# Attention and experts on one core: the first key unit of a chunk one slot ahead, and a reordered prologue

## What is computed

```python
x = x + _L0_xattn_ref(_layernorm(x), ctx, ctx, mask, Wq, bq, Wk, bk, Wv, bv, Wo, bo)
x = x + _L0_ffn_ref(_layernorm(x), Wr, W1, b1, W2, b2)

# attention
q = (q_in @ Wq + bq).reshape(bs, q_len, h, d).transpose(0, 2, 1, 3)
k = (k_in @ Wk + bk).reshape(bs, k_len, h, d).transpose(0, 2, 1, 3)
v = (v_in @ Wv + bv).reshape(bs, k_len, h, d).transpose(0, 2, 1, 3)
score = einsum('bhqd,bhkd->bhqk', q, k) / sqrt(d)
attn = softmax(where(mask, -1e+30, score))
out = einsum('bhqk,bhkd->bhqd', attn, v) @ Wo + bo

# experts
probs = softmax(einsum('bsd,ed->bse', x, Wr))
topv, topi = top_k(probs, 2)
out = sum over e of combine[e] * (gelu(x @ W1[e] + b1[e]) @ W2[e] + b2[e])
```

## Time and profile before

| | us |
|---|---|
| median of 3 runs | 906.77 |
| lowest, highest | 905.45, 907.99 |
| the profiled execution | 904.83 |
| its span | 903.0 |
| TensorE busy | 760.7 (84%) |
| VectorE busy | 670.0 (74%) |
| ScalarE busy | 621.2 (69%) |
| GpSimd busy | 477.3 (53%) |
| mean TensorE clock granted, as a share of full | 0.943 |

### The profile page before, as it was taken

The page is one execution under the profiler, slowest core; times in us unless marked ns, Lnnn a source line. Parts: engine busy times, 40 slices in busy tenths (PEclk is TensorE's granted clock), DMA queues, the critical chain, the costliest instruction groups (busy, mean ns, idle before and its releaser), DMA issues.

```text
span 903.0 us, 19629 instructions
## 1 busy us (share of the span) xinstructions
PE 760.7 (84%) x5606; PEld 546.5 (61%) x5606; DVE 670.0 (74%) x2133; ACT 621.2 (69%) x1131; POOL 477.3 (53%) x715
## 2 busy tenths in 40 slices
PE   2689899998998988889988889759999999999700
PEld 1456555655655655656665665448888888888500
DVE  3568888888888887888887887557777777777536
ACT  4667677677677676667776677458888888888500
POOL 4122665565565565454453453453777777767720
PEclk9599999999999999999999999759999999999955
DMA  5333355455445445334243233388877777877059
GB/s 157 75 83 73 98 129 150 115 135 153 115 127 154 116 130 145 102 93 100 72 100 92 70 85 80 141 281 274 253 250 236 254 240 244 243 225 246 19 205 353
DMA packets 117887, 140.33 MB, mean 155 GB/s; under 512 B 20431, under 2 KB 76134, under 8 KB 117799
## 3 DMA queue, kind: packets, MB, share of 16 engines
q1 hardware_dynamic: 105079, 115.72, 45.6%
q0 software_dynamic: 9088, 17.07, 5.4%
q10 hardware_dynamic: 3632, 6.49, 1.9%
HBM read 73.40 MB, written 36.08 MB: 121 GB/s over the span
## 4 chain that ended last, share of the span: by engine, by line
PE 52%; DMA 14%; DVE 13%; SPq 10%; ACT 4%; issue 4%; POOL 1%; POOLq 0%; DVEq 0%; ACTq 0%
DMA kb<-ks 9%; SPq L346 9%; PE bank L1247 6%; DVE mx L700 5%; PE bank L1269 4%; PE bank L1415 4%; PE bank L1412 4%; PE bank L1429 4%; PE bank L1413 4%; PE bank L1427 4%; PE bank L1428 4%; PE bank L1229 3%; DVE ks L695 3%; DMA qb<-yd 3%; PE bank L1257 2%
## 5 line engine op out<-in xcount | busy, mean ns | idle before, releaser
L630 POOL DMA_INDIRECT yd<-vs,idt x156 | 164.9, 1057 | 79.5 <-DVE vs L978 41.0
L1048 ACT ACTIVATE pt<-bank,mpair 120x512 f32<-120x512 f32 x256 | 172.2, 688 | 42.5 <-PE bank L1257 42.3
L531 POOL DMA_INDIRECT xd<-rows,posi x128 | 130.6, 1020 | 127.4 <-DVE posi L777 73.0
L700 DVE TENSOR_REDUCE mx<-bank 128x4 f32<-128x480 f32 x256 | 157.7, 648 | 38.4 <-PE bank L1247 38.2
L964 DVE TENSOR_TENSOR qb<-hid,qb 128x512 fp32r<-128x512 f32 x156 | 109.4, 702 | 68.3 <-ACT hid L1164 67.0
L1161 ACT ACTIVATE qb<-bank,btile 128x512 fp32r<-128x512 f32 x156 | 107.6, 690 | 34.0 <-PE bank L1429 25.0
L1247 PE MATMUL bank<-kb,qs 128*128 128x480 f32 x256 | 96.7, 431 | 35.9 <-DMA kb<-ks 24.9
L1269 PE MATMUL bank<-pt,vs 120*32 120x128 f32 x2048 | 111.4, 290 | 13.3 <-ACT pt L1048 10.3
L1257 PE MATMUL bank<-qb,ks 128*120 128x512 f32 x256 | 118.3, 482 | 2.6 <-DMA qb<-negm 2.6
L1164 ACT ACTIVATE hid<-bank,btile 128x512 f32<-128x512 f32 x156 | 106.3, 681 | 0.0
L1247 PEld LDWEIGHTS bank<-kb,qs 128*128 128x128 f32 x256 | 47.3, 194 | 72.0 <-DMA kb<-ks 34.5
(11 more groups left out here) (200 smaller groups left out, 1940.1 us busy)
## 6 DMA issues: line engine op xcount, KB each, us to landing
kb<-wd SPq DMA_DIRECT2D x40, 512.0 KB, 5.1
qb<-wd SPq DMA_DIRECT2D x38, 512.0 KB, 5.0
qb<-qs SPq DMA_DIRECT2D x128, 112.0 KB
kb<-ks SPq DMA_DIRECT2D x128, 105.0 KB
rows<-xd SPq DMA_DIRECT2D x39, 264.0 KB, 2.8
wd<-wsp SPq DMA_DIRECT2D x16, 512.0 KB, 3.8
qb<-yd SPq DMA_DIRECT2D x16, 512.0 KB, 6.0
xd<-zrows SPq DMA_DIRECT2D x8, 528.0 KB, 4.6
```

The costliest lines, as they stand in the source:

```text
L531: g.indirect_dma_start(xd, bass.IndirectOffsetOnAxis(ap=posi[r.phase][:, bk:bk + 1], axis=0), rows[r.phase][:, bk // 2, bk % 2, :], None, ...
L630: g.indirect_dma_start(yd, bass.IndirectOffsetOnAxis(ap=idt[k][:, j:j + 1], axis=0), yrow[p.parity][:, j, :], None, bounds_check=2 * NTOK ...
L700: v.tensor_reduce(mx[:, b, gg, :], wide[(4 + u) % 3][:, 0:J * KL].rearrange("p (j k) -> p j k", j=J), op=ALU.max, axis=AX.X).then_inc(w_fr ...
L1048: a.activation(pt[t % NP][:].rearrange("p j q -> p (j q)"), scores[t % 2][0:KL, :], ACT.Exp, bias=mpair[s.parity][:, t // G:t // G + 1], s ...
```

## The change

**Unit 0 one slot ahead.** Key unit 0 of chunk n+2 is projected at the end of slot n, behind the last `weigh` and ahead of the transpose of the maxima. ScalarE halves it at the end of slot n too, ahead of `take_heads` of sequence 1. VectorE subtracts it behind the negated maxima and ahead of the router's top 2, with a wait for the last `by_key`, since `ks` of that parity is read there. Units 1 to 3 stay. Slot -1 does this for chunk 1; chunk 0 has both key units in slot -2.

**Prologue.** TensorE projects both key units of chunk 0 ahead of the first transposes of x. ScalarE splits the key weights ahead of issuing the zero DMA of kb, then clears qb of parity 0, norms, halves unit 0, lays out the query weights, halves unit 1. The clearing of the other pair moves from the end of slot -1 to ahead of its `norm_x`. VectorE folds the biases first, subtracts unit 0, and only then prepares the masks. SyncE loads the biases ahead of the mask. GpSimd's constants (`fill`) move from the start of slot -1 to slot -2, behind the split of the context.

SyncE, prologue:

```diff
             load_x(At(0, 0))
             load_ctx(At(0, 0))
-            sp.dma_start(masku[:, :], mask).then_inc(mask_in, 16)
             for k, b in enumerate((bq, bk)):
                 sp.dma_start(bqk[:, k, :], b.rearrange("(a n) -> a n", a=1).to_broadcast([P, D])).then_inc(bias_in, 16)
+            sp.dma_start(masku[:, :], mask).then_inc(mask_in, 16)
```

GpSimd, its slot:

```diff
-                if n == -1:
-                    fill()
...
                     g.tensor_tensor(xcTl[k][:, tc], xcT[k][:, tc], xcTh[k][:, tc], ALU.subtract).then_inc(hl_done, 1)
+                    if n == -2:
+                        fill()
```

VectorE, its slot (`unsplit` now takes the chunk as an argument and stands outside `slot`):

```diff
                 if exists(n, 1):
-                    unsplit(0)
                     route(1)
-                    unsplit(1)
+                    if n != -1:
+                        unsplit(c, 1)
...
                     v.scalar_tensor_tensor(negm[k][:, 1, :], nsrc, -1.0, negm[k][:, 0, :], ALU.mult, ALU.subtract).then_inc(nm_split, 1)
+                if exists(n, 2) and n >= -1:
+                    if n >= 0:
+                        dve.wait_ge(b_full, s.count(8, 8))
+                    unsplit(c + 1, 0)
```

VectorE ahead of the slots, where the mask instructions move from ahead of the biases to behind the first new line:

```diff
+            unsplit(At(0, 0), 0)
             dve.wait_ge(mask_in, 32)
...
             v.tensor_tensor(wq3[1][:], wst[1][:], wq3[0][:], ALU.subtract).then_inc(prep, 1)
+            unsplit(At(0, 0), 1)
```

ScalarE ahead of the slots (the lines that lay out and split the query weights move to between the two new halvings):

```diff
+            act.wait_ge(wk_in, 16)
+            a.activation(wk3[0][:], wst[0], ACT.Copy).then_inc(wst_hi, 1)
             act.wait_ge(zero_src, 1)
             dst, src = clear(kb[0], "p g j n")
             act.dma_start(dst.bitcast(F32), src).then_inc(kb_zero, 16)
-            act.wait_ge(wk_in, 16)
-            a.activation(wk3[0][:], wst[0], ACT.Copy).then_inc(wst_hi, 1)
...
+            a.activation(*clear(qb[0], "p b g j q"), ACT.Copy).then_inc(blk_zero, 1)
...
             norm_x(At(-1, 1), -3)
+            halve(At(0, 0), 0, -1)
...
+            halve(At(0, 0), 1, -1)
             slots(act, slot)
```

ScalarE, its slot:

```diff
-                if exists(n, 1):
-                    halve(c, 0, n)
+                if exists(n, 1) and n != -1:
                     halve(c, 1, n)
...
+                        if n == -1:
+                            a.activation(*clear(kb[1], "p g j n"), ACT.Copy).then_inc(blk_zero, 1)
+                            a.activation(*clear(qb[1], "p b g j q"), ACT.Copy).then_inc(blk_zero, 1)
                         if exists(n, 3):
                             norm_x(s, n)
...
+                if exists(n, 2) and n >= -1:
+                    halve(c + 1, 0, n + 1)
                 if exists(n, 0):
                     take_heads(s, 1, n)
```

TensorE, its slot:

```diff
-                if exists(n, 1):
-                    project(c, 0, n)
+                if n == -2:
+                    project(s + 2, 0, -1)
+                    project(s + 2, 1, -1)
...
-                if exists(n, 1):
+                if exists(n, 1) and n != -1:
                     project(c, 1, n)
...
+                    if exists(n, 2) and n >= -1 and t == 7:
+                        project(c + 1, 0, n + 1)
                     if exists(n, 1) and t == 7:
                         pe.wait_ge(w_free, c.count(12, 12))
```

More of the change, by code:

```diff
@@ L674, in residual, with unsplit @@
                 v.tensor_tensor(xb, small[1][:, 0:D], xb, ALU.add).then_inc(x1_done, 1)
+            def unsplit(c, u):
+                k = c.parity
+                dve.wait_ge(w_part, c.count(4, u + 1))
+                gs = slice(2 * (u % 2), 2 * (u % 2) + 2)
+                if u < 2:
+                    views = ks[k][:, gs, :], *(w[:, 0:2 * KW].rearrange("p (g n) -> p g n", g=2)[:, :, 0:K2]
+                                               for w in (wide[u % 3], part[u % 2]))
+                else:
+                    views = qs[k][:, :, gs, :], *(w[:, 0:2 * N2].rearrange("p (g b q) -> p b g q", g=2, b=2)
+                                                  for w in (wide[u % 3], part[u % 2]))
+                v.tensor_tensor(*views, ALU.subtract).then_inc(w_free, 1)
             def slot(s, n):
@@ L683, in slot @@
                     dve.wait_ge(pv_done, s.count(8))
-                def unsplit(u):
-                    dve.wait_ge(w_part, c.count(4, u + 1))
-                    gs = slice(2 * (u % 2), 2 * (u % 2) + 2)
-                    if u < 2:
-                        views = ks[k][:, gs, :], *(w[:, 0:2 * KW].rearrange("p (g n) -> p g n", g=2)[:, :, 0:K2]
-                                                   for w in (wide[u % 3], part[u % 2]))
-                    else:
-                        views = qs[k][:, :, gs, :], *(w[:, 0:2 * N2].rearrange("p (g b q) -> p b g q", g=2, b=2)
-                                                      for w in (wide[u % 3], part[u % 2]))
-                    v.tensor_tensor(*views, ALU.subtract).then_inc(w_free, 1)
                 def best(u):
@@ L823, in slot @@
                 if exists(n, 1):
-                    unsplit(2)
-                    unsplit(3)
+                    unsplit(c, 2)
+                    unsplit(c, 3)
                 if exists(n, 2):
@@ L908, in _ @@
             v.tensor_tensor(wk3[1][:], wst[0][:], wk3[0][:], ALU.subtract).then_inc(prep, 1)
-            dve.wait_ge(mask_in, 32)
-            put(v.tensor_copy(maskg[:, :], masku[:, :]))
-            put(v.tensor_copy(mcol[:, :], maskuT[:, :]))
             dve.wait_ge(bias_in, 32)
@@ L1147, in _ @@
             norm_x(At(-1, 1), -3)
+            halve(At(0, 0), 0, -1)
+            act.wait_ge(wst_zero, 1)
+            act.wait_ge(z_done, 1)
+            zsrc = zq[:].rearrange("p (h d) -> p h d", h=H)
+            for c in range(3):
+                a.activation(wst[1][:].rearrange("p g j r -> p (g j) r")[:, :, 8 * c:8 * c + 8], zsrc, ACT.Copy).then_inc(wst_done, 1)
+            a.activation(wst[1][:].rearrange("p g j r -> p (g j) r")[:, :, BLO:BHI + 1],
+                         zk[:].rearrange("p (h d) -> p h d", d=1).to_broadcast([P, H, 2]), ACT.Copy).then_inc(wst_done, 1)
+            act.wait_ge(wst_done, 4)
+            a.activation(wq3[0][:], wst[1][:], ACT.Copy).then_inc(wst_hi, 1)
+            halve(At(0, 0), 1, -1)
             slots(act, slot)
```

22 lines of the change are left out of this document (6 added, 16 removed).

## The result

Beside each other on one chip, the changed kernel took 933.12 us (median of 4, 930.73 to 935.19) and the kernel before 906.11 (median of 4, 904.01 to 907.99). The ratio is 1.0287, with a 95% interval of 1.0243 to 1.0331. The profiled execution took 930.73, with a span of 928.9 (before 904.83 and 903.0). The prediction was 925 with a range of 911 to 936: the direction is right, the size is 8 us short.

What follows compares the result with a forecast made beforehand. TensorE is busy through almost all of a slot, so its waits count, the largest for the key blocks. 904.8 - 9.0 (prologue) + 27.1 (loop) = 922.9, plus 1.9 for the median, 924.8, said as 925; range 911 to 936.

Steps and rivals of the forecast that it cites:

- the chain and the step that lengthens it: Slot boundary: head transposes, key unit 1, halving, subtraction, key DMAs, max matmul; ots behind unit 0's halving delays it 0.93 us.
- The five terms: From attention matmuls' end to head transposes: unit 0, halving's start, next ScalarE instruction, ots, transposes' start; 2.43 us against 1.50.
- The plain slot: Loop slot without GpSimd's weight split; the forecast for a usual slot was 0.93 less 0.05, 0.88 us longer.
- The rival in which half is given back: Loop: the wait for key blocks shrinks and returns 0.4 to 0.6 us per boundary; 913 us, chance 0.15.
- the hold: GpSimd's weight split blocking VectorE in 16 slots: 0.4 us longer or shorter each, 6.9 in all, counted as zero.
- The prediction's sentence by that rule: In slots with a weight split, the next two-input VectorE instruction would be caught instead; sum some 7 us higher.
- the prologue: Start of the kernel through slot 0: keys projected earlier and clearing moved; 9.0 us less, bounds 7 and 11.
- Unit 0 of chunk 1: Prologue: it stands ahead of the next maxima transpose at half clock and takes back 0.4 us.
- slot 0's: Slot 0: maxima to attention matmuls 2.1 us less, from there to max matmul 0 to 2.4 less; 3.2 taken.
- the prediction's upper bound of 0.15: Loop: VectorE's subtraction of unit 0 makes the heads late; counted at nothing, at most 0.15 us per slot.
- the rival "more is lost": Loop: GpSimd's mask copy late, port lost in 16 slots, or TensorE's clock lower; 7 to 14 us more, chance 0.2.
- The prediction's rival for the intended gain: Loop: key DMAs leave earlier and the wait for key blocks goes; another 18 us less, 880, chance 0.04.

Runs made afterwards that it cites:

- Experiment 3: The kernel before, with only ots of sequence 1 copied later, behind the next slot's first halving; 1011.04 us in one run.
- Experiments 5: The changed kernel with GpSimd's weight split moved from ahead of the row copies to behind them; 956.67 us, 1.020 times the kernel before.
- experiment 9: The kernel before with the new prologue only, and GpSimd's weight split moved behind a slot's fourth scatter; 895.56 us, 0.988 times the kernel before.
- experiment 10: The new prologue with the loop of the kernel before, run a second time; 898.96 us, 0.9925 times the kernel before.
- experiment 2: The new prologue with the loop of the kernel before, first run; 943.66 us beside 948.01 for the kernel before.
- experiment 7: The changed kernel with ots copied ahead of the halving and VectorE's subtraction of unit 0 back in the next slot; 943.03 us in one run.
- experiment 1: The changed kernel with ots of sequence 1 copied ahead of the halving of unit 0; 962.03 us, 1.016 times the kernel before.

## Why the prediction came out as it did

**Right: the chain and the step that lengthens it.** The forecast named the head transposes as the point at which both paths begin, and the halving of unit 0 ahead of ots as what delays them. The five terms sum to 2.43; measured is 2.40. The wait for ots was to be some 0.9, and is 0.96. The plain slot was to be 0.88 longer, and is 17.26 less 16.38, 0.88. The terms hold one by one too: the halving starts 1.02 after unit 0 (0.98 said), ots 0.65 behind it (0.62), takes 0.59 (0.60), and the transposes follow 0.14 later (0.23). Experiment 3 shows the one-for-one rule with nothing but ots moved. The rival in which half is given back is out: the wait for the key blocks fell by 1.5 us over the whole run.

**Right by its bound, wrong in the sum: the hold.** The step read "in the sum it is zero", with 6.9 us as its bound; measured are 5.3, 0.33 in each of 16 slots. I knew from the earlier trace rows that an operation in 16 slots was held, and estimated that the split moves 0.4 later against the maxima. It moved 0.50 later (1.41 less 0.91). The step that failed is to call that a toss-up. It could have been a gain only if the end of GpSimd's subtraction did not set the slot, and the trace of before shows that it did: 13 slots at 17.11 to 17.17, wherever yy fell in the subtraction. So the 0.50 goes into the slot, less what VectorE has less to do behind the hold. Where yy is held, the extra over the 0.88 is 0.48. Where `before` is held instead, it is 0.33. Experiments 5 and 9 show that this hold is a cost of the split's place.
The Trainium skill's page "SBUF — State Buffer", section "Who interferes with whom", says that whoever comes first keeps the shared pair for its whole instruction, and that two inputs from SBUF are enough for VectorE to need it. The trace agrees in all 16 split slots of the changed kernel: each has one such operation that ends with GpSimd's subtraction. The prediction's sentence by that rule, some 7 us more, was nearer than its own zero, but not by its route: the slots in which the next operation is caught (18.33) are shorter than those in which yy is (18.48).

**Mis-sized: the prologue.** 9.0 was predicted and 6.9 measured, just under its lower bound of 7. The first max matmul is 5.6 earlier (6.2 said): the second norm starts at 16.83 and the DMA issue follows at 18.18, not 17.6. Unit 0 of chunk 1 cost 0.3 (0.4 said). The term that failed is slot 0's, 3.2 said and 1.6 measured. Its first half held (5.15 where 5.1 was said). Its second, "3.9 at full clock, as slot 1 has it", did not: the key blocks landed 6.27 after their issue, and that stretch took 5.23. That is 1.1 less than before, as much as the sum had taken for it. What the sum put at nothing is the rest of the slot: the wait for the blocks was followed by 5 us at a granted clock of 0.66, and the rest took 8.04 instead of 6.55, 1.5 more. That this happened is partly chance. With the same prologue and the old loop, and the clock at 1.00 in slot 0, slot 0 took 17.16 and 17.48 (experiments 10 and 2), 2.9 and 2.5 less than before.

**Counted at nothing, and rightly in the sum.** The heads wait 0.47 instead of 0.22, which is over the prediction's upper bound of 0.15 for it, but the chain to the key DMAs did not grow (2.84 against 2.82). The extra wait came out of the wait for the key blocks, which in the undisturbed plain slots fell from 0.57 to 0.35. The mask copy on GpSimd is at 162.75, and the attention matmuls wait for the first exponential 0.32, as in the kernels with the old loop; that half of the rival "more is lost" did not come. Its other half did: the hold in 16 slots. Its third part, the clock, came at four boundaries of the loop and in slot 0.

In all, 7.8 us are missing from the profiled sum (922.9 said, 930.73 measured): 5.3 for the hold, 2.1 for the prologue, 0.8 behind the attention stage, less 0.4 elsewhere in the loop; the medians add 0.5. The prediction's rival for the intended gain would have needed unit 1 earlier; experiment 7 shows that, even with ots and the subtraction out of the way, no slot gets shorter.

## What to carry to other kernels

Before work is moved ahead of a boundary, find the instruction from which both the busy engine's path and the DMA chain start, and ask of each engine's queue what now stands ahead of that instruction's inputs. A step that waits for the moved work holds up all that is queued behind it, and the delay goes through one for one. And where GpSimd runs a long two-input operation over VectorE's small ones, place it by the trace, where nothing with two SBUF inputs is on the path. If the slots with that operation all have one length, wherever the held operation falls in it, its end sets the slot, and whatever delays GpSimd's queue is paid in full. Here the end came 0.50 later against the rest and cost a slot 0.33 to 0.48 us, and a better place took 0.34 off it.

## What the runs showed of the hardware

- A VectorE addition of bf16, 8 columns wide and 0.15 us long, took up to 1.27 us beside GpSimd's 128x512 subtraction of 1.28 us. In each of the changed kernel's 16 split slots the held operation ended within 0.03 us of that subtraction's end. Fused operations with two such inputs are held too: vyy (L714) took 345 ns in the mean in experiment 1, 154 in experiment 2.
- TensorE's granted clock fell behind single waits in an otherwise busy loop: after 1.36 and 1.49 us in the cases above. In experiment 9 a wait of 1.98 for the key blocks made its slot 19.65 long, with a clock of 0.78 in the stretch below. But in experiment 10 waits of 1.73 and 1.78 left slots of only 17.5 and 17.6, and behind the changed kernel's waits of 0.96 it fell at four of 30 boundaries in one trace and at one (218.25) in the other. What else decides it stays open.

```profile
328.22 0.71 PE L1253 MATMUL bank<-kb,qs 128*128 128x480 f32 x2 [1.98 <-DMA kb<-ks]
```

```profile
330.00:336.50 6.50, 6.25 (x50) 3.34 (x48) 4.81 (x15) 4.19 (x10) 1.89 (x5) 0.78 0.53 158
```

- The key blocks landed 5.25 us after their issue in most slots and 6.3 in slot 0. What makes that difference stays open.
